# Four loads in place of three for parameters and contexts, on two DMA queues, in a gated cross-attention block

## What is computed

```
query  = ctx @ Wq.T + bq          # [4, 256, 128]
key    = ctx @ Wk.T + bk
attn   = softmax(query @ key.T)   # [4, 256, 256]
x      = x + tanh(g_xattn) * (layernorm(x) @ attn.T)
h      = layernorm(x) as e4m3
x      = x + tanh(g_ffn) * ((gelu(h @ w_gating[0]) * (h @ w_gating[1])) as e4m3 @ w_linear)
```

## Time and profile before

| what | us |
|---|---|
| median of 3 runs | 49.52 |
| lowest, highest | 49.23, 51.98 |
| the profiled execution, its own time | 49.34 |
| span of its instructions | 47.5 |
| busy: PE | 41.6 |
| busy: DVE | 34.7 |
| busy: ACT | 29.5 |

### The profile page before, as it was taken

How to read it: one execution, slowest core, us unless ns; L and a number is a source line. 1 busy time by engine, 2 the same in 40 slices (tenths; PEclk the granted TensorE clock), 3 DMA queues, 4 the chain that set the end, 5 groups by cost and what they waited for, 6 DMA issues and landing times.

```text
span 47.5 us, 841 instructions
## 1 busy us (share of the span) xinstructions
PE 41.6 (87%) x246; PEld 28.6 (60%) x246; DVE 34.7 (73%) x110; ACT 29.5 (62%) x67; POOL 16.8 (35%) x35
## 2 busy tenths in 40 slices
PE   3998999963999999998999999999999999999000
PEld 1317788833787888863435556665645888895000
DVE  0101099999798979899999991787669977999700
ACT  0902947299798799755599749775557495463000
POOL 3204994039999641600610170000000059802300
PEclk9999999999999999999999999999999999999999
DMA  0499999999999960000000000000000001460092
GB/s 0 79 365 326 317 367 369 195 203 203 170 114 104 106 61 1 0 0 21 0 0 0 0 0 0 0 0 7 0 0 0 0 14 64 163 215 0 0 340 102
DMA packets 3460, 4.64 MB, mean 98 GB/s; under 512 B 384, under 2 KB 2176, under 8 KB 3456
## 3 DMA queue, kind: packets, MB, share of 16 engines
q1 hardware_dynamic: 2304, 3.48, 21.5%
q0 software_dynamic: 864, 0.79, 17.7%
q10 hardware_dynamic: 288, 0.33, 2.2%
HBM read 5.90 MB, written 1.05 MB: 146 GB/s over the span
## 4 chain that ended last, share of the span: by engine, by line
PE 65%; DVE 13%; DMA 9%; ACT 2%; SPq 2%; issue 1%; DVEq 1%
PE bank L645 15%; PE bank L639 15%; PE bank L599 14%; PE bank L664 13%; DMA x_sb<-x 9%; DVE st L413 6%; PE bank L571 4%; DVE nmax L420 2%; PE bank L621 2%; DVE yo L486 2%; DVE mv L416 2%; PE bank L564 2%; SPq L211 2%; DVE attn L431 1%; ACT xq L344 1%; ACT ys L402 1%
## 5 line engine op out<-in xcount | busy, mean ns | idle before, releaser
L471 DVE SCALAR_TENSOR_TENSOR ap<-bank,gl 128x512 f16<-128x512 f32 (+1 forms) x20 | 11.6, 582 | 3.4 <-PE bank L645 1.8
L353 ACT ACTIVATE gl<-bank 128x512 bf16<-128x512 f32 (+1 forms) x20 | 10.0, 509 | 5.5 <-PE bank L639 5.4
L639 PE MATMUL bank<-xq,wg 128*128 128x512 fp8e4 (+1 forms) x40 | 10.2, 337 | 0.2 <-ACT xq L344 0.2
L645 PE MATMUL bank<-xq,wg 128*128 128x512 fp8e4 (+1 forms) x40 | 10.2, 337 | 0.0
L664 PE MATMUL bank<-wl,aq 128*128 128x256 fp8e4 x64 | 9.6, 273 | 0.0
L599 PE MATMUL bank<-attnT,xT_sb 128*128 128x256 f32 x32 | 8.1, 385 | 0.0
L664 PEld LDWEIGHTS bank<-wl,aq 128*128 128x128 f16 x64 | 6.2, 98 | 2.4 <-DVE aq L480 0.2
L280 POOL TENSOR_TENSOR yo<-ys,x 128x256 f32<-128x256 f32 x4 | 2.8, 730 | 10.3 <-ACT ys L361 10.3
L599 PEld LDWEIGHTS bank<-attnT,xT_sb 128*128 128x128 f32 x32 | 5.6, 190 | 0.7 <-ACT attnT L327 0.2
L265 POOL TENSOR_TENSOR r<-ve,neg_half 128x2 f32<-128x2 f32 x4 | 3.0, 760 | 8.5 <-DVE ve L454 8.5
L480 DVE TENSOR_SCALAR aq<-ap 128x512 uint16<-128x512 uint16 (+1 forms) x20 | 5.8, 292 | 0.0
(11 more groups left out here) (50 smaller groups left out, 54.4 us busy)
## 6 DMA issues: line engine op xcount, KB each, us to landing
x_sb<-x SPq DMA_DIRECT2D x4, 256.0 KB, 4.6
xT_sb<-xT SPq DMA_DIRECT2D x4, 256.0 KB, 7.1
out<-yo SPq DMA_DIRECT2D x5, 128.0 KB, 1.7
wg<-w_gating POOLq DMA_DIRECT2D x4, 128.0 KB, 8.6
par<-params_ctxT SPq DMA_DIRECT2D x1, 256.0 KB, 3.2
wl<-w_linear POOLq DMA_DIRECT2D x2, 128.0 KB, 11.0
out<-yo SPq DMA_DIRECT2D x1, 256.0 KB, 2.0
par<-params_ctxT SPq DMA_DIRECT2D x1, 194.0 KB, 2.9
```

The source lines that it names most:

```text
L353: nc.scalar.activation(gl[:, s % 2, toks], gate_b[s % 2][:, toks], ACT.Gelu_apprx_tanh).then_inc(gelu_ready, 1)
L471: nc.vector.scalar_tensor_tensor(ap[:, s % NAP, toks], up_b[s % 2][:, toks], ACT_SCALE, gl[:, s % 2, toks], ALU.mult, ALU.mult).then_inc(p ...
L639: mm = nc.tensor.matmul(gate_b[s % 2][:, toks], wg8[:, c, k, 0, o:o + P], xq[:, g, k, toks], start=(k == 0), stop=(k == KC - 1))
L645: mm = nc.tensor.matmul(up_b[s % 2][:, toks], wg8[:, c, k, 1, o:o + P], xq[:, g, k, toks], start=(k == 0), stop=(k == KC - 1))
```

## The change

`params_ctxT` and `par` keep their layout; the cut between columns 132 and 388 is new. So there are four pieces: 0 (66 KB, query weight, biases, gates) and 2 (192 KB, key weight and context 1) issued by SP; 1 (128 KB, context 0) and 3 (256 KB, contexts 2 and 3) issued by ACT. The waits follow: `project_q(0)` for pieces 0 and 1, `project_k(0)` and POOL's weight loads for piece 2, `project_q(2)` and `project_q(3)` for piece 3. Tanh of the gates still waits for piece 0 alone.

```
-    CUTS = (0, P + 4 + L, NPAR + 2 * L, NPAR + 4 * L)
+    CUTS = (0, P + 4, P + 4 + L, NPAR + 2 * L, NPAR + 4 * L)
...
-            pool.wait_ge(s_ctx[1], 16)
+            pool.wait_ge(s_ctx[2], 16)
...
-            cols = slice(CUTS[1], CUTS[2])
-            act.dma_start(par[:, cols], params_ctxT[:, cols]).then_inc(s_ctx[1], 16)
+            for c in (1, 3):
+                cols = slice(CUTS[c], CUTS[c + 1])
+                act.dma_start(par[:, cols], params_ctxT[:, cols]).then_inc(s_ctx[c], 16)
...
-                if b != 1:
-                    pe.wait_ge(s_ctx[min(b, 2)], 16)
+                if b == 0:
+                    pe.wait_ge(s_ctx[0], 16)
+                    pe.wait_ge(s_ctx[1], 16)
+                if b >= 2:
+                    pe.wait_ge(s_ctx[3], 16)
...
-                    pe.wait_ge(s_ctx[1], 16)
+                    pe.wait_ge(s_ctx[2], 16)
```

## The result

The changed kernel takes 49.67 us (median of 21 runs, 49.33 to 51.13) against 49.52 (21 runs): ratio 1.0066, 95% interval 1.0039 to 1.0092. By the ratio it is slower by 0.3 us, by the medians by 0.15. The time lies in the range; its sign is the wrong one, since 0.1 us of gain was forecast. Ratios here are of the executions up to 1.5% above the fastest of their kernel; medians have all of them. Five of the 21 took 50.57 to 51.13, where of the 21 of before a single one took over 50.2 (51.98); no trace is of one of these. The profiled execution took 49.52, with a span of 47.7.

What follows compares the result with a forecast made beforehand. The prediction took the first load of x, then DVE, then PE as the bound. For the profiled execution 49.34 + 0 + 0.03 - 0.1 = 49.27 us; for the median it said 49.4, range 48.9 to 50.0.

Steps and rivals of the forecast that it cites:

- What bounds the kernel: Chain to the end: first load of x landing at 5.88, DVE's statistics, then PE from 11.48; shifts pass nearly one to one.
- The first term: Bytes moved until x's last byte: 898 KB before and after, so 0 us.
- The second term: The new load ahead of x: 128 more packets, 8 per engine, bounds 0 to 0.49 us, taken as 0.03 us loss.
- The third term: At the handover from parameters to x, piece 3 on the other queue may fill the rate's fall: gain of 0.1 us.
- the dip: Rate falling for 0.3 us from 341 to 143 GB/s as traffic goes from parameters to x; alone worth 0.17 us.
- The projections: PE's early stage: first projection from 3.5, first key projection about 4.6, energies ending about 7.0 instead of 6.87; no effect.
- The slack of 1.63 us: Sequence 0's energies end at 6.87, DVE reads them at 8.50; taken as slack of the whole projection stage.
- Rival three: Key weight late, piece 2 starved by piece 3, so energies become the bound; 50.5 at the very worst; chance 0.03.
- Rival two: First load of x later through more packets ahead on each DMA engine, 32 for 24: 0.49 us, 50.0; chance 0.15.

Runs made afterwards that it cites:

- more packets: Kernel before, contexts 2 and 3 set 4 columns apart, so the same single 256 KB load has 256 packets of 1 KB, not 128 of 2 KB: ratio 0.9975.
- small first piece: Kernel before with its three loads recut to 66 KB (SP), 320 KB (ACT) and 256 KB (SP): ratio 0.9974.
- late key: Kernel before, but the first key projection also waits for the first load of x: ratio 1.0035, median 50.61 against 49.35.
- two loads: Kernel before with pieces 0 and 1 joined on SP, x behind them, contexts 2 and 3 on ACT: ratio 0.9993, median 50.35 against 49.54.
- cut alone: The change's four pieces, but piece 3 stays on SP's queue ahead of x; against the kernel before, ratio 1.0175, and 1.0246 when run again.
- late cut: Kernel before with contexts 2 and 3 as two loads of 128 KB, both from SP: ratio 1.0103.
- move alone: Kernel before with its three pieces, but ACT issues the last (contexts 2 and 3, 256 KB): ratio 0.9944, and 0.9935 when run again.
- swap: The change with pieces 2 and 3 exchanged between queues (SP issues 0 and 3, ACT 1 and 2); against the kernel before, ratio 1.0089.
- eight warm-ups: The change with eight warm-up matmuls in place of six; against the kernel before, ratio 1.0104.
- change again: The changed kernel run once more without edit, for a second trace and interval; against the kernel before, ratio 1.0057.

## Why the prediction was wrong, point by point

**What bounds the kernel** was right. The landing of x, the statistics of DVE and the first transpose are the chain, and the law of 37.86 us shows that a shift goes through one to one. That the time lies in the range is in part luck: a loss and a gain, each larger than forecast, nearly cancel.

**The first term**, no more bytes ahead of x, was right as bytes.

**The second term failed: "the new load itself: 128 more packets", taken as 0.03 us between 0 and 0.49.** It was priced by packets, and those cost nothing (0.9975). What costs is that four loads stand ahead of x where three stood: every one of the nine comparisons with four or five is at 1.0057 or above, every one of the ten with three or two at 1.0039 or below, among them one with more packets and one with a small first piece. By medians two of the ten are slow as well, the late key and the two loads, where the projections come late. Later issue of x can't be the whole cause: six of the nine issue x at 1.64 or sooner. The cut alone measured 0.0175 to 0.0246 of 49.5, 0.9 to 1.2 us, beyond my upper end of 0.49, and the late cut 0.5 us; how much of that is the issue of x at 2.10 in place of 1.64 is open. The rates show how: the same bytes move slower. From 2.40 to 6.40 the nine traces with four or five loads moved 981 to 1337 KB, the eleven with three or two 1315 to 1543. Why the engines move them slower after a fourth load is open; no view here names what a slow packet waits for.

**The third term, a gain of 0.1 us from filling the dip, had the right sign and was too small.** The move alone gains 0.0056 to 0.0065, 0.3 us. From the cut alone to the change the move of piece 3, with x issued sooner, is worth more, 1.0175 or 1.0246 to 1.0066, that is 0.5 to 0.9 us. So the change is a loss of about 0.9 to 1.2 and a gain of about 0.5 to 0.9, and 0.3 us of loss is left. That the dip is where the gain comes from is argued, not shown. One reading beside it was wrong: that one queue alone moves 341 GB/s and two 366. From 3.4 to 4.4 the kernel before moved 367 GB/s, all of it on SP's queue:

```profile
q1 hardware_dynamic: 195, 0.37, 105.1%
```

I weighed the sum against the rule of the Trainium skill ("DMA: Bandwidth & Descriptors", "Issuing engines are not separate DMA queues") that only issue time is saved. The move alone speaks against taking it as the whole: x is issued 0.5 us sooner there, but landed 0.9 us sooner in the trace above.

**The projections** were right in their starts (tanh 3.07 for 3.2, the first key projection 4.62 for 4.6) and wrong in their pace. I took 0.59 us for each; the first two took 1.2, and the energies end at 7.96. The slack of 1.63 us was misread as well: I measured it at the row maximum, where 0.7 were left, but PE's own way to the first transpose ends its cover sooner, 1.16 us of idle time before and 0.23 after. POOL came at 4.88 for 4.6, without effect. Rival three was given 0.03 because I let only the landing of piece 2 decide; by half pace the projections did decide in the traces of the swap, the two loads, the small first piece and the move alone. How much of the change's time they make was not settled: neither of its two traces shows it, eight warm-ups did not bring the 1.006 back, and the five executions above 50.5 have no trace.

**Rival two** had the sign, and 0.49 us of loss for 0.3; its mechanism, packets ahead of x, is refuted by the run with more packets.

## What to carry to other kernels

Price an added load by a run, not by its packets or bytes: here a fourth load ahead of the critical one cost more than anything it brought early. A transfer that the chain starts with was helped by moving another off its queue, without cutting it. And before an early operand is worth anything, look at the pace at which the engine will use it: PE started sooner and finished later. Look for slack at every place where the stage is waited for, not only at the first.

## What the runs showed of the hardware that was not expected

PE's pace at the start is not to be read from the granted clock, which reads 1.00 in all of these stretches. Behind the warm-up and 0.23 us of idle time the projections of before took 0.97 us for the first and 0.59 for the next. Those of the change follow the warm-up without idle time and took 1.19, 1.22 and 1.03 before the fourth took 0.61; in the trace of the change again it was 1.19, 0.87 and then 0.59. In the swap, with 0.77 us of waiting after the first one, they took 1.06 to 1.22 until past 8 us. So idle time just before is not the whole reason; what sets the pace is open.

Of two executions of one kernel, the cut alone, with 2.45 and 2.55 us of idle time of PE before the first transpose, one was followed by a granted clock of 0.50, 1.2 GHz, from 14 to 17 us, and the other by none. So an early delay can be paid for a second time, or not.
